# The sixteen experts of a routed layer taken in reverse order

## The chip, the cores and the metric

The kernel runs on one core of a Trainium2 chip. The metric is the device time of one launch in microseconds (us), the median of several launches. TensorE (PE) multiplies matrices, VectorE (DVE), ScalarE (ACT) and GpSimd (POOL) do the elementwise work, and DMA queues move data between HBM and on-chip memory. Each engine runs its own instructions in program order and waits at semaphores.

## The reference, cut to what matters

A block of three layers on 1,024 tokens of width 512 in float32: a cross attention, a self attention, and a mixture of experts. The change is in the last:

```python
scores = sigmoid(x @ gate_weight.T)              # 16 experts in 4 groups of 4
biased = scores + expert_bias                    # 2 of 4 groups by the sum of their two best
_, sel = top_k(where(group kept, biased, -inf), 4)   # 4 experts per token, ties to the lower number
w = 2.5 * scores[sel] / sum(scores[sel])
for e in range(16):                              # g, u: 256 x 512, d: 512 x 256
    y = (silu(x @ g[e].T) * (x @ u[e].T)) @ d[e].T
    out += w_of_e * y
out += shared expert                             # the same form, for every token
```

The inputs are drawn with a fixed seed, with a bias per expert that makes the load uneven. Working the routing out on them gives the number of tokens per expert:

| expert | 0 | 1 | 2 | 3 | 4 | 5 | 6 | 7 | 8 | 9 | 10 | 11 | 12 | 13 | 14 | 15 |
|---|---|---|---|---|---|---|---|---|---|---|---|---|---|---|---|---|
| tokens | 981 | 544 | 973 | 306 | 335 | 60 | 4 | 360 | 0 | 6 | 10 | 0 | 304 | 2 | 211 | 0 |
| tiles of 128 rows | 8 | 5 | 8 | 3 | 3 | 1 | 1 | 3 | 1 | 1 | 1 | 1 | 3 | 1 | 2 | 1 |
| tiles up to and with it | 8 | 13 | 21 | 24 | 27 | 28 | 29 | 32 | 33 | 34 | 35 | 36 | 39 | 40 | 42 | 43 |

An expert without tokens still gets one tile: the kernel counts an expert's tiles as the number of steps of 128 below its count, and the first step is written as -1.

## The kernel before, in words

The attention layers fill the first 1,080 us and are untouched. The last layer is `build_moe`, in two parts.

**Routing.** Eight groups of 128 tokens are projected, normalised and turned. For each, DVE works out which 4 experts every token takes: `route_groups` and `route_experts` count for each expert how many others are better, with `tri` (a 16 by 16 table of 0 and 1 in the constants `route_rows`) deciding ties. POOL then scatters each token's row to four places in an HBM buffer `xs`, in which every expert owns eight blocks of 128 rows. `table_cols` and `table_row` turn the counts into a table of 47 tiles (`tab`): for each tile the expert whose weights it needs, the place of these weights, and the block of `xs` to read. 47 is the most that can be needed; the tiles beyond the 43 real ones read and write spare blocks.

**The tile loop.** For each tile, in the order of the table, PE first waits for the tile's weights (`pe.wait_ge(w_ready, ready)`), then does the gate and up products (12 products of 512 columns on `XT`), in their midst turns the hidden rows of the tile before (`turn_h`) and the input rows of the next (`turn_x`), and then does the down products of the tile before (6 products of 512 columns). ACT and DVE split the operands into a high and a low part in between: DVE does `ht_low` (L1830), `xt_low` (L1820), `gated` (L1826) for each tile, and in tiles 8 to 16 also one step each of `sort_slots` (L1743 to L1755), which sorts each token's four places. SP writes each tile's result back to its block of `xs`. Below, tile i begins with the first of its gate products, an L64 row of PE, and "the ht_low of tile i" is DVE's L1830 of that tile, which runs within tile i + 1.

**Weights.** On-chip memory holds five experts (`NSLOT = 5`, slot e % 5). POOL brings them in by number: for each expert it waits until the expert five before it is through (`tile_done` against `cum_i`), makes the high part (L1523), the low part (L1480), raises `w_ready`, and issues the load of the expert two further on (L1484) into one of two raw buffers. Expert 0 is made by ACT and DVE before the loop; experts 2 to 4 need the shared expert's last product.

```python
pool.wait_ge(tile_done, pool.value_load(cum_i[0:1, e - NSLOT:e - NSLOT + 1], min_val=1,
                                        max_val=NTILE + 1))
...
pool.tensor_copy(slot(e)[0], raw[(e + 1) % 2]).then_inc(pool_hi, 1)
```

**The end.** After its last expert POOL issues 32 gathers (L1539): for k = 0 to 3 the row of each token's k-th expert in the order of number, eight groups of tokens each. The eight of one k wait until the tiles of expert 12 + k are written back, since a token's k-th expert can't have a higher number. DVE adds each gathered group to the output, weighted (`combine`, L1837): twelve of them within the last tiles, 20 after the `ht_low` of the last tile; SP then writes the eight output groups (L1454).

Of the kernel before, what the change touches and what calls it, by code (L numbers as in the profile page):

```python
# [25 lines left out]
ALU = mybir.AluOpType  # L26
# [29 lines left out]
NE, TOPK, NG, TOPG, I = 16, 4, 4, 2, 256  # L56
# [786 lines left out]
def wait(eng, sem, value):  # L843

    if not isinstance(value, int) or value > 0:
        eng.wait_ge(sem, value)
# [418 lines left out]
C_BIAS, C_TRI, C_TRIG, C_DIAG = 0, NE, NE + NE * NE, NE + NE * NE + NG * NG  # L1265
# [8 lines left out]
def _route_rows(bias):  # L1274

    tri = (np.arange(NE)[None, :] < np.arange(NE)[:, None]).astype(np.float32)
    tri_g = (np.arange(NG)[None, :] < np.arange(NG)[:, None]).astype(np.float32)
    slot = np.arange(NE) % NSLOT
    step = np.where(np.arange(NE) == NE - 1, 0, np.where(slot == NSLOT - 1, 1 - NSLOT, 1)) * SLOT
    real = (np.arange(NE) < NE - 1).astype(np.float32)  # L1280
    parts = [bias, tri.ravel(), tri_g.ravel(), -1e30 * np.eye(GS).ravel(), np.arange(TOPK), np.arange(NE) * T,
             np.arange(NT) * P - (np.arange(NT) == 0), step, real]
    return np.concatenate([np.asarray(p, np.float32) for p in parts]).reshape(1, C_END)


def build_moe(nc, ctx, sem, t, keep):
# [7 lines left out]
    def sb(name, shape, dt=F32):  # L1294
        return ctx.enter_context(nc.sbuf_tensor(name, shape, dt))
# [22 lines left out]
    masked, cmp_e, rank = sb("masked", [P, NE]), sb("cmp_experts", [P, NE, 2, NE]), sb("rank", [P, NE])  # L1318
# [20 lines left out]
    def c_row(at, n):  # L1339
        return con[:, at:at + n]  # L1340

    tri = c_row(C_TRI, NE * NE).rearrange("p (i j) -> p i j", j=NE)
    tri_g = c_row(C_TRIG, NG * NG).rearrange("p (i j) -> p i j", j=NG)
    diag = c_row(C_DIAG, GS * GS).rearrange("p (i j) -> p i j", j=GS)

    pb = [ctx.enter_context(nc.psum_tensor(f"bank{j}", [P, BANK], F32)) for j in range(8)]
# [8 lines left out]
    A = [early[:, j * nh * P:(j + 1) * nh * P].rearrange("p (h x) -> p h x", x=P) for j in range(2)]  # L1355
# [271 lines left out]
    def _(dve):  # L1627
        count = [0]

        def link(ins):  # L1630

            count[0] += 1
            ins.then_inc(route, 1)
            dve.wait_ge(route, count[0])

        def free(ins):

            count[0] += 1
            ins.then_inc(route, 1)
# [47 lines left out]
        def route_experts(tt):  # L1687
            j = tt % 2
            mj = masked[:].unsqueeze(1).to_broadcast([P, NE, NE])
            mi = masked[:].unsqueeze(2).to_broadcast([P, NE, NE])  # L1690
            free(dve.tensor_tensor(cmp_e[:, :, 0, :], mj, mi, ALU.is_gt))  # L1691
            link(dve.tensor_tensor(cmp_e[:, :, 1, :], mj, mi, ALU.is_equal))
            link(dve.tensor_tensor(cmp_e[:, :, 1, :], cmp_e[:, :, 1, :], tri, ALU.mult))
            link(dve.tensor_reduce(rank[:], cmp_e[:].rearrange("p i a j -> p i (a j)"), AX.X, ALU.add))
            wait(dve, prefix_mm, tt - 1)
            link(dve.tensor_scalar(sel[j][:], rank[:], float(TOPK), None, ALU.is_lt))
            wait(dve, prefix_mm, tt)
            dve.tensor_tensor(seen[1 - j][:], seen[j][:], sel[j][:], ALU.add).then_inc(sel_made, 1)
            link(dve.tensor_tensor(K[j][:], rank[:].unsqueeze(1).to_broadcast([P, TOPK, NE]),
                                   c_row(C_K, TOPK).unsqueeze(2).to_broadcast([P, TOPK, NE]), ALU.is_equal))  # L1700
            link(dve.tensor_tensor(kx[:], K[j][:], sig[:, tt, :].unsqueeze(1).to_broadcast([P, TOPK, NE]), ALU.mult))
            link(dve.tensor_reduce(wk[:], kx[:], AX.X, ALU.add))
            link(dve.tensor_reduce(wsum[:], wk[:], AX.X, ALU.add))
            link(dve.tensor_scalar(wsum[:], wsum[:], 1e-20, None, ALU.add))
            link(dve.reciprocal(wsum[:], wsum[:]))
            link(dve.tensor_scalar(cw[:, tt, :], wk[:], wsum[:, 0:1], SCALING, ALU.mult, ALU.mult))
# [71 lines left out]
        for tt in range(NT):  # L1778
            x2_stats(tt)
            if tt >= 2:  # L1780
                slots(tt - 2)
            norm(tt)
            if tt == NT - 1:
                break
            if tt >= 1:
                route_groups(tt - 1)
            h3_low(tt)
            if tt >= 1:
                route_experts(tt - 1)
            if tt == 1:  # L1790
                dve.wait_ge(sh_hi, 1)
                dve.tensor_tensor(WS[:, shared + wcol:shared + 2 * wcol], raw[0], f32(WS[:, shared:shared + wcol]),
                                  ALU.subtract).then_inc(sh_lo, 1)
        last = NT - 1
        h3_low(last)
        route_groups(last - 1)
        route_experts(last - 1)
        route_groups(last)
        product(0)
        route_experts(last)  # L1800
        product(1)
        hidden_low(0)
# [211 lines left out]
def build(nc, t):  # L2014

    outer = ExitStack()
    with outer:
# [37 lines left out]
        with ExitStack() as ctx:  # L2055
            build_moe(nc, ctx, sem, t, keep)
# [35 lines left out]
def _rows(w):  # L2092

    return w.T.reshape(w.shape[1] // P, P, w.shape[0]).transpose(1, 0, 2)
# [50 lines left out]
```

## Time and profile before

| | us |
|---|---|
| median of 3 runs | 1516.76 |
| lowest and highest | 1516.18, 1520.94 |
| the profiled execution | 1518.74 |
| its span, from the first to the last instruction | 1516.9 |
| mean granted TensorE clock over the span | 0.959 of full |

The profiled execution took 1.84 us more than its span, and 1.98 us more than the median. Times in the views are from the start of the span. Of the span, the last 433 us are `build_moe`'s, and the tile loop starts at 1247.58 us and ends with DVE's last `ht_low` at 1486.97 us.

### The profile page before, as it was taken

The page shows a single profiled execution, that of the slowest core. Times are in us where ns is not written, and L with a number is a line of the kernel's source. Part 1 is how long each engine was busy: PE and PEld are TensorE (multiplying, and loading weights), DVE is VectorE, ACT ScalarE, POOL GpSimd, SP SyncE. Part 2 cuts the span into 40 slices and gives each one's busy share as a digit, 9 for nine tenths or more (in the row PEclk, how much of TensorE's full clock was granted, in tenths as well). Part 3 has the DMA queues.
Part 4 walks back from the last instruction along what each step waited for, and adds up shares of the span by engine and source line. Part 5 has one row for each costly group of instructions (what it writes and reads, how often), then busy time and mean ns, then how long its engine had stood idle before and what let it go on. Part 6 is the DMA issues. An engine that isn't in the chain of part 4 may idle for free. (4 is left out here: it accounts for less than half of the span.)

```text
span 1516.9 us, 22837 instructions
## 1 busy us (share of the span) xinstructions
PE 1361.9 (90%) x7136; PEld 1105.5 (73%) x7136; DVE 809.9 (53%) x1371; ACT 734.6 (48%) x1741; POOL 573.7 (38%) x346
## 2 busy tenths in 40 slices
PE   5998699999999999999985899999689979999992
PEld 4776578777777777777764688888578768777781
DVE  4434365656566666666544444444479863433235
ACT  2444465655555555555533577777521213333330
POOL 2122333333333332333103233333246466517985
PEclk9999799999999999999997999999699999999996
DMA  5786540323232323232315111112544246446667
GB/s 192 244 274 184 221 153 29 136 87 124 97 124 97 124 97 124 97 124 97 135 60 190 62 50 63 49 48 98 190 163 142 84 174 215 155 139 219 232 205 232
DMA packets 78984, 209.79 MB, mean 138 GB/s; under 512 B 5888, under 2 KB 39168, under 8 KB 72960
## 3 DMA queue, kind: packets, MB, share of 16 engines
q1 hardware_dynamic: 69472, 163.78, 30.4%
q0 software_dynamic: 7136, 38.80, 7.7%
q10 hardware_dynamic: 2304, 6.29, 1.1%
q8 instruction: 40, 0.66, 0.2%
q14 instruction: 32, 0.26, 0.1%
HBM read 154.59 MB, written 92.01 MB: 163 GB/s over the span
## 5 line engine op out<-in xcount | busy, mean ns | idle before, releaser
L660 DVE TENSOR_TENSOR probsT_lo<-psTr,probsT_hi 128x512 fp32r<-128x512 f32 x256 | 176.5, 690 | 199.9 <-ACT probsT_hi L610 199.5
L610 ACT CAST probsT_hi<-psTr 128x512 fp32r<-128x512 f32 x256 | 149.8, 586 | 211.7 <-PE psTr L750 211.0
L750 PE MATMUL psTr<-ident,probs 128*128 128x128 f32 x1024 | 152.5, 276 | 18.6 <-DVE probsT_lo L660 12.4
L750 PEld LDWEIGHTS psTr<-ident,probs 128*128 128x128 f32 x1024 | 122.3, 141 | 62.0 <-DVE probsT_lo L660 28.8
L527 POOL TENSOR_TENSOR ctxT_lo<-ctx_f,ctxT_hi 128x512 fp32r<-128x512 f32 x32 | 41.3, 1290 | 321.1 <-ACT ctxT_hi L579 321.1
L655 DVE TENSOR_REDUCE nmax<-psS 128x1 f32<-128x1024 f32 x128 | 155.4, 1214 | 11.5 <-PE psS L66 10.7
L572 ACT ACTIVATE probs<-psS,nmax 128x1024 f32<-128x1024 f32 x128 | 143.3, 1120 | 28.2 <-DVE nmax L655 28.2
L64 PE MATMUL bank<-w_slots,ao_first_hi 128*128 (+1 forms) x252 | 107.8, 428 | 15.3 <-DVE w_slots L1774 9.4
L64 PE MATMUL psV<-probsT_hi,kv_hi 128*128 128x512 f32 x256 | 117.3, 458 | 2.0
L64 PE MATMUL psS<-kT_hi,qe 128*128 128x512 f32 x256 | 113.1, 442 | 5.5 <-issue 4.7
L1480 POOL TENSOR_TENSOR w_slots<-w_ahead,w_slots 128x3072 fp32r<-128x3072 f32 x15 | 102.5, 6836 | 1.2
L66 PE MATMUL psS<-kT_hi,qe 128*128 128x512 f32 x256 | 102.5, 400 | 0.0
L65 PE MATMUL psS<-kT_lo,qe 128*128 128x512 f32 x256 | 101.6, 397 | 0.0
L66 PE MATMUL psV<-probsT_hi,kv_lo 128*128 128x512 f32 x256 | 101.3, 396 | 0.0
L65 PE MATMUL psV<-probsT_lo,kv_hi 128*128 128x512 f32 x256 | 100.5, 392 | 0.0
L66 PE MATMUL bank<-w_slots,ao_first_lo 128*128 (+1 forms) x252 | 100.1, 397 | 0.0
L65 PE MATMUL bank<-w_slots,ao_first_hi 128*128 (+1 forms) x252 | 99.6, 395 | 0.0
L64 PE MATMUL bank<-w_slots 128*128 128x512 f32 (+1 forms) x206 | 84.9, 412 | 8.1 <-DVE w_slots L1830 4.4
L1186 PEld LDWEIGHTS psSs<-kTs,qT 128*128 128x128 f32 x512 | 76.4, 192 | 9.6
L1830 DVE TENSOR_TENSOR w_slots<-bank,w_slots 128x256 fp32r<-128x256 f32 x47 | 19.9, 424 | 117.0 <-ACT w_slots L1608 116.9
L66 PE MATMUL bank<-w_slots 128*128 128x512 f32 (+1 forms) x206 | 82.2, 399 | 0.0
L65 PE MATMUL bank<-w_slots 128*128 128x512 f32 (+1 forms) x206 | 82.0, 398 | 0.0
(268 smaller groups left out, 3328.8 us busy)
## 6 DMA issues: line engine op xcount, KB each, us to landing
w_ahead<-w_exp POOLq DMA_DIRECT2D x14, 1536.0 KB, 7.4
qe<-stage SPq DMA_DIRECT2D x16, 1024.0 KB, 6.7
qe<-qe SPq DMA_DIRECT2D x16, 1024.0 KB, 5.0
wraw<-w_pairs SPq DMA_DIRECT2D x8, 1792.0 KB, 11.3
early<-xs SPq DMA_DIRECT2D x47, 256.0 KB, 2.7
xs<-h_rows SPq DMA_DIRECT2D x47, 256.0 KB, 2.0
early<-ctx SPq DMA_DIRECT2D x16, 512.0 KB, 3.8
ao<-attn_out SPq DMA_DIRECT2D x32, 256.0 KB, 2.4
```

What stands on the lines that cost most here:

```text
L64: pe.matmul(out, lhs[0], rhs[0], start=start, stop=False, skip_group_check=True)
L65: pe.matmul(out, lhs[0], rhs[1], start=False, stop=False, skip_group_check=True)
L66: return pe.matmul(out, lhs[1], rhs[0], start=False, stop=stop, skip_group_check=True)
L527: pool.tensor_tensor(CT.lo[:, cols[0], cols[1]], CX[:].rearrange("p (h s) -> p h s", s=S), f32(CT.hi[:, cols[0], cols[1]]), ALU.subtract). ...
L572: act.activation(PR[np_][:, rt, :], psS[rt % 2][:], ACT.Exp, bias=nmax[np_][:, rt:rt + 1], accum_out=rsum[np_][:, rt:rt + 1]).then_inc(exp ...
L610: act.copy(PT[k % PTN].hi[:], psT[slot][:]).then_inc(turned_hi, 1)
L655: dve.tensor_reduce(nmax[np_][:, rt:rt + 1], psS[rt % 2][:], AX.X, ALU.max, negate=True).then_inc(max_made, 1)
L660: dve.tensor_tensor(out, psT[slot][:], f32(hi), ALU.subtract).then_inc(turned_free, 1)
L750: last = pe.transpose(psT[slot][:, q * P:(q + 1) * P], src(q), ident[:])
L1186: last = pe.matmul(psS[j][:, h, :], QB[j][:, h].rearrange("p b s -> p (b s)"), KB[kt][:, g, :], start=False, stop=h == REP - 1, skip_group ...
L1480: pool.tensor_tensor(slot(e)[1], raw[(e + 1) % 2], f32(slot(e)[0]), ALU.subtract).then_inc(w_ready, 1)
L1830: dve.tensor_tensor(HT[i % 2][1], psHT[i % 2][:, 0:I].rearrange("p (k x) -> p k x", k=NIT), f32(HT[i % 2][0]), ALU.subtract).then_inc(ht_l ...
```

## The change: experts in reverse order

The kernel's expert number j now stands for the reference's expert 15 - j: the weights, the router's columns and the bias are handed over reversed. So that ties still go to the same expert, the comparisons read the tie tables transposed. No instruction is added, removed or moved on any engine.

```diff
@@ build_moe
     tri = c_row(C_TRI, NE * NE).rearrange("p (i j) -> p i j", j=NE)
-    tri_g = c_row(C_TRIG, NG * NG).rearrange("p (i j) -> p i j", j=NG)
+    tri_after = c_row(C_TRI, NE * NE).rearrange("p (j i) -> p i j", j=NE)
+    tri_g = c_row(C_TRIG, NG * NG).rearrange("p (j i) -> p i j", j=NG)
...
@@ route_experts
-            link(dve.tensor_tensor(cmp_e[:, :, 1, :], cmp_e[:, :, 1, :], tri, ALU.mult))
+            link(dve.tensor_tensor(cmp_e[:, :, 1, :], cmp_e[:, :, 1, :], tri_after, ALU.mult))
...
@@ kernel
-    gates = np.concatenate([A(L0_ffn_shared_gate)[None], A(L0_ffn_gate_proj)])
-    ups = np.concatenate([A(L0_ffn_shared_up)[None], A(L0_ffn_up_proj)])
-    downs = np.concatenate([A(L0_ffn_shared_down)[None], A(L0_ffn_down_proj)])
+    gates = np.concatenate([A(L0_ffn_shared_gate)[None], A(L0_ffn_gate_proj)[::-1]])
+    ups = np.concatenate([A(L0_ffn_shared_up)[None], A(L0_ffn_up_proj)[::-1]])
+    downs = np.concatenate([A(L0_ffn_shared_down)[None], A(L0_ffn_down_proj)[::-1]])
...
-        "gate_w": _rows(A(L0_ffn_gate_weight)),
-        "route_c": _route_rows(A(L0_ffn_expert_bias)),
+        "gate_w": _rows(A(L0_ffn_gate_weight)[::-1]),
+        "route_c": _route_rows(A(L0_ffn_expert_bias)[::-1]),
```

The table of tiles that the device works out then reads, by the new numbers:

| expert | 0 | 1 | 2 | 3 | 4 | 5 | 6 | 7 | 8 | 9 | 10 | 11 | 12 | 13 | 14 | 15 |
|---|---|---|---|---|---|---|---|---|---|---|---|---|---|---|---|---|
| tiles | 1 | 2 | 1 | 3 | 1 | 1 | 1 | 1 | 3 | 1 | 1 | 3 | 3 | 8 | 5 | 8 |
| tiles up to and with it | 1 | 3 | 4 | 7 | 8 | 9 | 10 | 11 | 14 | 15 | 16 | 19 | 22 | 30 | 35 | 43 |

## Rows read from the trace of the kernel before

**Rows 1.** The page: busy us, share, instructions; then the chain that ended last.
```profile
PE 1361.9 (90%) x7136; PEld 1105.5 (73%) x7136; DVE 809.9 (53%) x1371; ACT 734.6 (48%) x1741; POOL 573.7 (38%) x346
...
PE bank L64 4%; PE bank L66 4%; PE bank L65 4%; POOL w_slots L1480 3%; POOL w_slots L1539 1%; POOL w_slots L1523 1%; PE bank L1950 1%; DVE cmp_experts L1691 1%; DVE h_rows L1660 1%; POOL w_ahead L1539 0%; PE bank L1981 0%; DVE st L1648 0%; DVE acc L1645 0%; DVE cmp_experts L1748 0%; DMA w_slots<-xs,slot_sorted_int 0%
```

**Rows 2.** Windows: stretch, its us, busy us (instructions) per engine, clock, DMA share.
```profile
1329.00:1487.00 158.00, 152.87 (x741) 122.44 (x739) 55.07 (x106) 59.51 (x124) 106.95 (x42) 0.99 0.60 201
1487.00:1517.00 30.00, 1.79 (x6) 1.06 (x6) 14.97 (x22) 0.58 (x1) 17.41 (x15) 0.53 0.74 228
```

**Rows 3.** Timeline of POOL, tile loop: start, us, work, idle before.
```profile
1246.22 2.74 POOL L1523 CAST w_slots<-w_ahead 128x3072 fp32r<-128x3072 f32 x1 [3.88 <-issue]
...
1256.70 2.77 POOL L1523 CAST w_slots<-w_ahead 128x3072 fp32r<-128x3072 f32 x1
...
1277.17 0.55 POOL L1484 DMA_DIRECT2D w_ahead<-w_exp  x1 [0.30 <-POOL w_slots L1480]
1290.95 2.75 POOL L1523 CAST w_slots<-w_ahead 128x3072 fp32r<-128x3072 f32 x1 [13.23 <-PE bank L66]
...
1358.25 2.75 POOL L1523 CAST w_slots<-w_ahead 128x3072 fp32r<-128x3072 f32 x1 [31.70 <-PE bank L66]
...
1387.43 2.75 POOL L1523 CAST w_slots<-w_ahead 128x3072 fp32r<-128x3072 f32 x1 [4.21 <-PE bank L66]
...
1422.81 6.78 POOL L1480 TENSOR_TENSOR w_slots<-w_ahead,w_slots 128x3072 fp32r<-128x3072 f32 x1
...
1441.20 2.75 POOL L1523 CAST w_slots<-w_ahead 128x3072 fp32r<-128x3072 f32 x1
...
1450.79 2.76 POOL L1523 CAST w_slots<-w_ahead 128x3072 fp32r<-128x3072 f32 x1
1453.63 6.86 POOL L1480 TENSOR_TENSOR w_slots<-w_ahead,w_slots 128x3072 fp32r<-128x3072 f32 x1
```

**Rows 4.** Timeline of PE: the first gate product of tiles 8, 16, 34 and 36.
```profile
1285.82 0.40 PE L64 MATMUL bank<-w_slots,ao_first_hi 128*128 x1
...
1328.36 0.49 PE L64 MATMUL bank<-w_slots,ao_first_hi 128*128 x1 [0.27 <-issue]
...
1417.79 0.40 PE L64 MATMUL bank<-w_slots,ao_first_hi 128*128 x1
...
1429.73 0.49 PE L64 MATMUL bank<-w_slots,ao_first_hi 128*128 x1 [2.08 <-POOL w_slots L1480]
```

**Rows 5.** Timeline of DVE: ht_low of tiles 7, 14, 15, 35, 36, and sort steps.
```profile
1288.04 0.42 DVE L1830 TENSOR_TENSOR w_slots<-bank,w_slots 128x256 fp32r<-128x256 f32 x1 [2.54 <-ACT w_slots L1608]
...
1295.14 0.28 DVE L1746 TENSOR_REDUCE slot_rank<-cmp_experts 128x32 f32<-128x128 f32 x1
...
1320.38 5.46 DVE L1748 TENSOR_TENSOR cmp_experts<-slot_rank,route_rows 128x128 f32<-128x128 f32 x1
1325.88 0.42 DVE L1830 TENSOR_TENSOR w_slots<-bank,w_slots 128x256 fp32r<-128x256 f32 x1
...
1330.73 0.42 DVE L1830 TENSOR_TENSOR w_slots<-bank,w_slots 128x256 fp32r<-128x256 f32 x1 [3.29 <-ACT w_slots L1608]
...
1432.60 0.42 DVE L1830 TENSOR_TENSOR w_slots<-bank,w_slots 128x256 fp32r<-128x256 f32 x1 [5.45 <-ACT w_slots L1608]
...
1438.44 0.42 DVE L1830 TENSOR_TENSOR w_slots<-bank,w_slots 128x256 fp32r<-128x256 f32 x1 [2.53 <-ACT w_slots L1608]
```

**Rows 6.** Windows, as in Rows 2, behind the wait of tile 36.
```profile
1430.00:1434.00 4.00, 4.00 (x15) 3.35 (x15) 0.75 (x2) 0.96 (x2) 3.78 (x3) 0.60 0.83 288
```

**Rows 7.** Timeline of POOL: the first and the last of the 32 gathers.
```profile
1461.93 1.04 POOL L1539 DMA_INDIRECT w_ahead<-xs,slot_sorted_int  x1 [1.44 <-issue]
...
1508.27 1.03 POOL L1539 DMA_INDIRECT w_slots<-xs,slot_sorted_int  x1 [0.30 <-issue]
```

**Rows 8.** Timeline of DVE: last ht_low, five additions in a row, the last addition.
```profile
1486.97 0.42 DVE L1830 TENSOR_TENSOR w_slots<-bank,w_slots 128x256 fp32r<-128x256 f32 x1
1487.31 3.40 DVE L1837 SCALAR_TENSOR_TENSOR acc<-w_slots,weight_sorted,acc 128x512 f32<-128x512 f32 x5
...
1513.45 0.75 DVE L1837 SCALAR_TENSOR_TENSOR acc<-w_slots,weight_sorted,acc 128x512 f32<-128x512 f32 x1 [0.52 <-DMA w_slots<-xs,slot_sorted_int]
```

**Rows 9.** Groups by line and form: busy us, mean ns, idle before.
```profile
L1693 DVE TENSOR_TENSOR cmp_experts<-cmp_experts,route_rows 128x256 f32<-128x256 f32 x8 | 3.4, 425 | 0.3
```

## The prediction

> **What bounds the kernel now.** I read the page first. PE is busy for 90% of the span, and the chain that ended last runs through PE's products, but three of POOL's lines are in it: the making of expert weights (L1523, L1480) and the gathers (L1539) [rows 1]. The windows say where. From 1329 to 1487 us, inside the tile loop, PE is busy 152.87 of 158 us; from 1487 us on it does 1.79 us of work in 30, while POOL and DMA work [rows 2]. So the loop is PE's, and the last 30 us are not.
>
> The timeline of POOL explains this end. With large experts in front, POOL waits for PE to free a slot: 13.23 us before expert 5 and 31.70 us before expert 7 [rows 3]. The small experts (numbers 8 to 11, a tile each) are used up faster than POOL makes weights. From expert 9 on it works without a break: expert 9 begins at 1387.43, expert 14 at 1441.20, expert 15 at 1450.79, and its low part ends at 1453.63 + 6.86 = 1460.49 [rows 3]. Only then come the gathers, the first at 1461.93 and the last at 1508.27 [rows 7], one every 46.34 / 31 = 1.49 us. DVE's last `ht_low` is at 1486.97, its last addition ends at 1513.45 + 0.75 = 1514.20, having waited for the gather [rows 8], and the span ends at 1516.9, 2.7 us later. From the last `ht_low` to the end it is 29.9 us, of which DVE adds for about half.
>
> **The change, part by part.** It issues nothing new. It changes the numbers in the tile table, and so who waits for whom. There are four terms.
>
> *The tie table.* L1693 runs eight times, 425 ns each [rows 9], and now reads the table with a stride of 16 elements. Nothing in the trace reads with this stride. The bounds are 0 and, if an element took twice the time, 8 x 0.42 = 3.4 us, all on DVE's path in the routing. The same line handles 256 elements in 0.42 us, one per 1.6 ns with its fixed cost, no faster form that the stride could spoil, so I take 0.
>
> *Starvation at the front of the loop.* The new order has 1, 2, 1, 3, 1, 1, 1, 1, 3, 1, 1 tiles for experts 0 to 10, so expert 11 is due at tile 16. POOL can start expert 5 at once, since expert 0's single tile is long done: at 1277.17 + 0.55 = 1277.72, where before it waited to 1290.95 [rows 3]; I take 1277.85 with the reading of the count. From there it never waits for a slot: expert e waits for the tiles of expert e - 5, for instance expert 11 for ten tiles, and these are through tens of us before it. The period, from start to start with the issue of a load, is (1441.20 - 1387.43) / 5 = 10.75 us [rows 3]. The shortest is 1256.70 - 1246.22 = 10.48. Expert 11 starts at 1277.85 + 6 x 10.75 = 1342.4, is ready 1453.63 + 6.86 - 1450.79 = 9.70 us after its start, at 1352.1, and PE starts 0.14 us after that (1429.73 against 1422.81 + 6.78 = 1429.59 [rows 3, 4]): tile 16 begins at 1352.2. Before, it began at 1328.36 [rows 4]. Hence **+23.8 us**.
>
> That tile 16 is the last that waits follows from the same sums: expert 12 is ready at 1362.8 for tile 19, which PE reaches at 1352.2 + 3 x 4.9 = 1366.9, and expert 13 at 1373.6 for tile 22. That the others don't add to it follows too. PE waits at tile 8 (expert 5 ready at 1287.6, PE there at about 1286 [rows 4]), and by about 5.8 us at each of tiles 9, 10 and 11, whose experts 6 to 8 come 10.75 us apart for one tile of 4.9 us; tile 11 begins at about 1319.9. From there to tile 16 it is five tiles, 24.5 us, in the 32.3 us that POOL takes for three experts: 7.8 us of slack, which must cover what follows.
>
> *Sort steps behind POOL.* In tiles 8 to 16 DVE does its sort steps. One of them, a product of two on-chip operands, took 5.46 us in place of 0.28 while POOL made a low part, and the next `ht_low` came at 1325.88, 7.67 us after the one before it in place of 4.9: 2.8 us lost [rows 5]. A reduction in the same position, with POOL in the midst of a low part, took 0.28 [rows 5]. So the steps that read two tensors (and the copy, for which I assume the same) wait for POOL's instruction to end, and PE loses what exceeds about 2.4 us. Before, POOL was idle in most of these tiles; now it is busy in all. Steps 3 and 5, in tiles 11 and 13, would lose 1 to 2 us each; step 7, in tile 15, ends with the same low part for which PE waits at tile 16. With the clock below this takes 4 to 5 of the 7.8 us of slack. **0 us**; uncovered they would cost up to 2.8 + 1.5 us.
>
> The Trainium skill (SBUF — State Buffer, Who interferes with whom) says that a Vector instruction with two on-chip inputs, or a copy in a two-port mode, and a GpSimd instruction exclude each other for their whole length, and that a reduction does not take part. The row of 5.46 us and that of 0.28 us agree; the copy isn't shown by a row here.
>
> *The clock after the wait.* PE idles some 3 us before tile 16. Behind the wait of tile 36 the granted clock was 0.60 over 4 us, that is, 1.2 GHz for most of them [rows 6]. The `ht_low` of tile 35 came 1432.60 - 1429.73 = 2.87 us after the tile's start, where at tile 8 it was 1288.04 - 1285.82 = 2.22, and the next 5.84 us later in place of 4.9 [rows 4, 5]: about **+1.5 us**, once, at tile 16. The earlier ones lie within waits for POOL.
>
> *From tile 16 to the last.* Before, this took 1486.97 - 1328.36 = 158.6 us. Tiles 16 to 34 took 89.4 us, 4.97 each; two tiles and a wait 11.9 us; from tile 36 to the last `ht_low` 57.2 us [rows 4, 8]. The wait at tile 36 and its slow clock are gone: expert 12 is now early. That is 11.9 - 9.8 = 2.1, and 1.5 of clock, **-3.6 us**. Tiles 16 to 34 ran with weight loads beside most of them; now loads end by about 1373. I take **-1.4 us** (0 to -2). So the last `ht_low` comes at 1352.2 + 158.6 + 1.5 - 3.6 - 1.4 = 1507.3, which is **+20.3 us**.
>
> *The end.* POOL makes its last weights by about 1395 and issues the gathers of k = 0 then. Those of k = 1, 2 and 3 wait for tile 29, 34 and 42 to be written back. Tile 42 is written back about 9 us after tile 43 starts (down products, ACT's copy, SP's write), at about 1494, and eight gathers at 1.49 us end by 1506, before DVE's last `ht_low`. The additions then wait for nothing: 20 of them at 3.40 / 5 = 0.68 us [rows 8], 13.6 us, then 2.7 us as before. The end comes 0.34 + 13.6 + 2.7 = 16.6 us after the last `ht_low`, 16.8 with some queueing of eight writes issued 0.68 us apart, in place of 29.9: **-13.1 us**.
>
> The sum is +20.3 - 13.1 = +7.2 us, which I round down to +7.0, since the period may lie nearer to 10.5. The span becomes 1523.9 and its execution 1525.7. Against the median of 1516.76, which lies 1.98 below the profiled execution, it is **1523.8 us**.
>
> The Trainium skill (Perfetto Trace Analysis, GPSIMD Engine Instruction) warns against the durations that a profile gives for GpSimd and advises the spacing of starts. By the durations alone an expert is 2.75 + 6.82 us, six of them 57.4 in place of 64.5, and the sum would be about 0. The spacing of 10.75 us contains the issue of a load and its idle gaps, and decides here.
>
> **Rivals.** A difference within 0.3%, 4.5 us, is about what a measurement of this kernel can't tell from no change.
>
> *The period is shorter, or the loop makes up more.* At 10.48 us tile 16 comes 1.6 us earlier; with no slow clock there, 1.5 us more, and with 4.85 us per tile behind it 0.6 more: +3.3, 1520.1. For it: 10.48 us was measured at the start of this very stretch [rows 3]. Against: the mean of five later periods is 10.75. With no gap at all, 9.6 us, the sum is 0. Chance 0.19.
>
> *The slack is not enough.* If the sort steps and slow clocks between tiles 11 and 16 take more than 7.8 us, or PE loses the clock for longer, or the stride costs, each adds on top: +4 on average, +11, 1528. For it: POOL is busy all the time there, and the steps come at an unknown phase of it. Chance 0.18.
>
> *The end isn't shortened.* If the gathers of the last expert still ended last, only the +20.3 would be left: 1537. It takes 13 us more than I find between the last write-back and the additions. Chance 0.03.
>
> *The other side: PE is never starved.* If POOL's weights were ready in time, only the end would change, by -13.1 (and -3.6 for tile 36): 1500 to 1504. It decides once expert 11 takes POOL below 8.5 us each, where POOL's two instructions alone take 9.6. As an escape from my sum, a gain needs 11.5 us less than I find in front. Chance 0.05.
>
> My forecast, +4.6 to +10, has the remaining 0.55. Slower holds 0.55 + 0.18 + 0.03 = 0.76, less a little at the edge: 0.75; same 0.20; faster 0.05. The range reaches down into the short period, 1518, and up over the lost slack, 1531.5.
>
> **What would show it.** POOL's casts for experts 5 to 15 follow each other every 10.5 to 10.9 us with no wait for PE, the last low part ending near 1395. PE waits for L1480 about six to eight times, by over 4 us at tiles 9, 10 and 11 and by 2 to 4 at tile 16, whose first product is near 1352; none after it. The granted clock drops between 1290 and 1360. The last `ht_low` is at 1505 to 1509, the gathers end before it, and the additions behind it stand without idle time. L1693 still takes 425 ns. The prediction is wrong if POOL's period changes with PE's idleness, if a sort step holds PE past tile 16, if PE's rate behind tile 16 differs from before, or if the routing before 1247 shifts.

## The result and the profile after

| | before | after |
|---|---|---|
| median, us | 1516.47 | 1537.66 |
| lowest and highest | 1515.16, 1520.94 | 1534.44, 1541.47 |
| profiled execution, its span | 1518.74, 1516.9 | 1535.88, 1534.1 |

The ratio is 1.013, with a 95% interval of 1.0099 to 1.0161: slower by 21 us, where the forecast was 7 and the range ended at 1531.5. Lines of the kernel after carry numbers one higher than before (`ht_low` L1831, low part L1481, cast L1524, gather L1540).

The page of after, as [rows 1] of before. POOL's low part now has 4% of the chain, before 3%, and the gathers are no longer among the lines shown:

```profile
PE 1374.0 (90%) x7136; PEld 1112.5 (73%) x7136; DVE 825.9 (54%) x1371; ACT 735.2 (48%) x1741; POOL 572.0 (37%) x346
...
POOL w_slots L1481 4%; PE bank L64 4%; PE bank L66 4%; PE bank L65 4%; POOL w_slots L1524 2%; PE bank L1951 1%; DVE cmp_experts L1692 1%; DVE h_rows L1661 1%; PE bank L1982 0%; DVE acc L1838 0%; DVE st L1649 0%; DVE acc L1646 0%; DVE w_slots L1775 0%; DVE w_slots L1766 0%
```

Windows of after, columns as in [rows 2], cut at the first `ht_low`, at that of tile 15, at the last, and at the end:

```profile
1257.20:1358.70 101.50, 80.96 (x360) 63.68 (x359) 45.48 (x53) 28.99 (x60) 95.86 (x30) 0.92 0.64 222
1358.70:1517.80 159.10, 152.22 (x732) 121.24 (x730) 55.06 (x106) 58.63 (x123) 68.23 (x42) 0.99 0.54 173
1517.80:1534.10 16.30, 1.63 (x6) 1.06 (x6) 13.65 (x21) 0.59 (x1) 0.00 (x0) 0.68 0.44 162
```

In the first stretch POOL is busy 95.86 of 101.5 us and PE waits for it: this stretch took 77.2 us before (from `ht_low` 1253.57 to that at 1330.73 [rows 5]). In the third DVE adds without a pause and POOL does nothing, where the same end took 29.9 us.

The timeline of POOL after, as [rows 3] and [rows 7]: the casts of experts 5 and 11, the last low part, the first and the last gather.

```profile
1281.89 2.75 POOL L1524 CAST w_slots<-w_ahead 128x3072 fp32r<-128x3072 f32 x1 [0.46 <-issue]
...
1345.85 2.75 POOL L1524 CAST w_slots<-w_ahead 128x3072 fp32r<-128x3072 f32 x1 [0.72 <-issue]
1348.68 6.76 POOL L1481 TENSOR_TENSOR w_slots<-w_ahead,w_slots 128x3072 fp32r<-128x3072 f32 x1
...
1390.51 6.83 POOL L1481 TENSOR_TENSOR w_slots<-w_ahead,w_slots 128x3072 fp32r<-128x3072 f32 x1
1398.78 1.04 POOL L1540 DMA_INDIRECT w_ahead<-xs,slot_sorted_int  x1 [1.44 <-issue]
...
1510.67 0.96 POOL L1540 DMA_INDIRECT w_slots<-xs,slot_sorted_int  x1 [0.30 <-issue]
```

The period is (1345.85 - 1281.89) / 6 = 10.66 us, and no cast waits for PE. The timeline of PE has the first product of tile 16, as [rows 4], and the waits of PE over the whole loop (us, times, longest) name the cause:

```profile
1355.58 0.49 PE L64 MATMUL bank<-w_slots,ao_first_hi 128*128 x1 [3.10 <-POOL w_slots L1481]
```
```profile
PE bank L64 <- POOL w_slots L1481: 17.3, 6, 5.5
PE bank L64 <- DVE w_slots L1831: 6.5, 2, 3.8
```

The timeline of DVE, as [rows 5] and [rows 8]: sort steps beside POOL's low parts, then the last tiles and the additions.

```profile
1296.13 6.03 DVE L1744 TENSOR_TENSOR cmp_experts<-slot_all 128x128 f32<-128x128 f32 x1
...
1308.05 0.28 DVE L1747 TENSOR_REDUCE slot_rank<-cmp_experts 128x32 f32<-128x128 f32 x1
...
1327.70 6.12 DVE L1752 TENSOR_TENSOR cmp_experts<-cmp_experts,slot_all 128x128 f32<-128x128 f32 x1
...
1342.23 2.08 DVE L1756 CAST slot_sorted_int<-slot_sorted 128x32 int32<-128x32 f32 x1
...
1358.73 0.42 DVE L1831 TENSOR_TENSOR w_slots<-bank,w_slots 128x256 fp32r<-128x256 f32 x1 [3.15 <-ACT w_slots L1609]
...
1504.07 0.42 DVE L1831 TENSOR_TENSOR w_slots<-bank,w_slots 128x256 fp32r<-128x256 f32 x1
...
1513.36 0.42 DVE L1831 TENSOR_TENSOR w_slots<-bank,w_slots 128x256 fp32r<-128x256 f32 x1 [4.42 <-ACT w_slots L1609]
...
1517.78 0.42 DVE L1831 TENSOR_TENSOR w_slots<-bank,w_slots 128x256 fp32r<-128x256 f32 x1 [1.02 <-ACT w_slots L1609]
1518.12 13.33 DVE L1838 SCALAR_TENSOR_TENSOR acc<-w_slots,weight_sorted,acc 128x512 f32<-128x512 f32 x20
```

Two `ht_low` near the end are 1513.36 - 1504.07 = 9.3 us apart in place of 4.8. ACT's timeline has the wait in front of it, which the view can't put down to an instruction of the program ("remote"). ACT waits there for the hidden rows of this tile to be turned, and PE's own row of that work stands more than 4 us earlier:

```profile
1508.31 0.38 PE L1982 MATMUL bank<-ident,early 128*128 128x128 f32 x2
...
1512.95 0.37 ACT L1609 CAST w_slots<-bank 128x256 fp32r<-128x256 f32 x1 [5.55 <-remote]
```

The semaphore events kept with the trace say the same. The one that PE raises behind this work came at 1512.93, where the record of the work ends at 1508.70, and the one behind the last gate product came at 1513.00, where its record ends at 1510.09. So what was late was PE's result or its signal, and not a transfer that ACT waited for. Why, the trace doesn't show. The ends of PE's records are modelled.

And the group of the tie product, as [rows 9]:

```profile
L1694 DVE TENSOR_TENSOR cmp_experts<-cmp_experts,route_rows 128x256 f32<-128x256 f32 x8 | 4.8, 605 | 0.3
```

The span grew by 17.2 us in four pieces: the first `ht_low` came 1257.17 - 1253.57 = 3.6 later; tile 16 began 1355.58 - 1328.36 = 27.2 later, that is 23.6 more; from there to the last `ht_low` it was 162.2 in place of 158.6, 3.6 more; the end was 13.6 shorter.

### The profile page after: what moved, and what is told of

Read it like the earlier page. It is cut to its first block and busy times, and to the rows that moved or that the text cites. A ratio compares the mean times of both kernels' runs of the same rounds, so it can differ in the third digit from the quotient of the medians.

```text
span 1534.1 us, 22837 instructions
## 1 busy us (share of the span) xinstructions
PE 1374.0 (90%) x7136; PEld 1112.5 (73%) x7136; DVE 825.9 (54%) x1371; ACT 735.2 (48%) x1741; POOL 572.0 (37%) x346
## 5 line engine op out<-in xcount | busy, mean ns | idle before, releaser
L64 PE MATMUL bank<-w_slots,ao_first_hi 128*128 (+1 forms) x252 | 110.1, 437 | 31.3 <-POOL w_slots L1481 17.3
L1481 POOL TENSOR_TENSOR w_slots<-w_ahead,w_slots 128x3072 fp32r<-128x3072 f32 x15 | 102.2, 6810 | 1.2
L65 PE MATMUL bank<-w_slots,ao_first_hi 128*128 (+1 forms) x252 | 101.6, 403 | 0.0
L66 PE MATMUL psS<-kT_hi,qe 128*128 128x512 f32 x256 | 101.5, 396 | 0.0
L64 PE MATMUL bank<-w_slots 128*128 128x512 f32 (+1 forms) x206 | 86.0, 417 | 11.6 <-DVE w_slots L1831 7.7
L1831 DVE TENSOR_TENSOR w_slots<-bank,w_slots 128x256 fp32r<-128x256 f32 x47 | 20.0, 425 | 125.4 <-ACT w_slots L1609 119.8
L64 PEld LDWEIGHTS bank<-w_slots,ao_first_hi 128*128 128x128 f32 x252 | 49.1, 195 | 51.7 <-issue 44.4
L66 PE MATMUL bank<-w_slots 128*128 128x512 f32 (+1 forms) x206 | 82.8, 402 | 0.0
```

The source lines that it names most:

```text
L64: pe.matmul(out, lhs[0], rhs[0], start=start, stop=False, skip_group_check=True)
L65: pe.matmul(out, lhs[0], rhs[1], start=False, stop=False, skip_group_check=True)
L66: return pe.matmul(out, lhs[1], rhs[0], start=False, stop=stop, skip_group_check=True)
L1481: pool.tensor_tensor(slot(e)[1], raw[(e + 1) % 2], f32(slot(e)[0]), ALU.subtract).then_inc(w_ready, 1)
```

## The experiments

The loop starts at different times in executions of one and the same kernel (the first `ht_low` at 1253.6 in before, but between 1247.9 and 1257.8 in the runs below), so I compare the stretch *L* from the first `ht_low` to the end of the span: 263.3 us in before, 276.9 in after. Ratios are against runs of the kernel before on the same chip. All `ht_low` times are from DVE's timeline. *L* varies too: with the order of before it was 263.3 us in before and 266.4 in the tables alone, so a difference of *L* between two single traces is good to about 3 us.

**The tables alone.** The kernel before with the transposed reads and nothing reversed.

```diff
+    tri_after = c_row(C_TRI, NE * NE).rearrange("p (j i) -> p i j", j=NE)
...
-            link(dve.tensor_tensor(cmp_e[:, :, 1, :], cmp_e[:, :, 1, :], tri, ALU.mult))
+            link(dve.tensor_tensor(cmp_e[:, :, 1, :], cmp_e[:, :, 1, :], tri_after, ALU.mult))
```

> The kernel before with only the tie tables read transposed (exact ties between experts go to the higher number). First theory: the table read with a stride of 16 elements costs 0.18 us in each of eight routing steps (0.606 against 0.425 us each), so the time is 1 to 2 us above before, and the tile loop starts 1 to 2 us later. Rival: the whole 3.6 us by which the changed kernel's tile loop started later comes from these reads, directly and by what queues behind them: 3 to 4 us above before. Second rival: neither, the start of the loop varies between executions by that much: no difference.

Measured: ratio 1.0005 (0.9983 to 1.0026). The product took 606 ns in place of 425. The stride does cost, 8 x 0.18 = 1.45 us, but that is less than a measurement of the whole can show.

**The tables stored the other way.** The kernel after, with the constants transposed so that L1694 reads without a stride; only `table_cols` then reads a tie table with one, once. (A second copy of the table beside the first does not fit in on-chip memory.)

```diff
-    parts = [bias, tri.ravel(), tri_g.ravel(), -1e30 * np.eye(GS).ravel(), np.arange(TOPK), np.arange(NE) * T,
+    parts = [bias, tri.T.ravel(), tri_g.T.ravel(), -1e30 * np.eye(GS).ravel(), np.arange(TOPK), np.arange(NE) * T,
...
-    tri_after = c_row(C_TRI, NE * NE).rearrange("p (j i) -> p i j", j=NE)
+    tri_after = c_row(C_TRI, NE * NE).rearrange("p (i j) -> p i j", j=NE)
...
```

> The changed kernel with the tie tables stored transposed, so that the routing reads them in order of address and only table_cols reads one with a stride, once. First theory (the stride costs 0.18 us in each of eight steps): L1694 back at 0.425 us, the tile loop starts 1 to 2 us earlier than in the changed kernel, time 1 to 2 us below it. Rival (the start of the loop varies by itself): no difference that can be measured.

The group of the product in this kernel:

```profile
L1694 DVE TENSOR_TENSOR cmp_experts<-cmp_experts,route_rows 128x256 f32<-128x256 f32 x8 | 3.4, 425 | 0.3
```

Ratio 1.0038 (1.0017 to 1.0058), L = 270.9. The 1.5 us of the stride are back in the row; the ratio can't be told from that of the kernel after on the same chip, which comes next.

**The kernel after again, on chips B and C.** No edit. (The chip of the first result isn't recorded; the tables alone, the mixed order's first run and the faster POOL in the reversed order ran on a chip A. The tables stored the other way, the late sort steps and the faster POOL in the order of before ran on chip B, and the last batch, from the second run of the mixed order on, on a chip D.)

> The changed kernel once more, with a trace of its own. If the time behind tile 16 (162 us to the last ht_low, where 155 were forecast) belongs to the order, it is 160 us or more again, with the same slow tiles beside the gathers; if the tile of 9.3 us at the end is an accident of one execution, it is 155 to 158 us. Ratio to before 1.010 to 1.016 in either case.

On chip B: 1524.4 us (12 runs, 1520.24 to 1528.21), ratio 1.0029 (1.0011 to 1.0047), L = 269.6. The ratio is below what I expected in either case. The end of DVE's timeline there:

```profile
1500.56 0.41 DVE L1831 TENSOR_TENSOR w_slots<-bank,w_slots 128x256 fp32r<-128x256 f32 x1
...
1505.54 0.42 DVE L1831 TENSOR_TENSOR w_slots<-bank,w_slots 128x256 fp32r<-128x256 f32 x1
...
1509.93 0.42 DVE L1831 TENSOR_TENSOR w_slots<-bank,w_slots 128x256 fp32r<-128x256 f32 x1
```

The tile of 9.3 us is one of 5.0, and no wait in this trace is put down to "remote". From the `ht_low` of tile 15 to the last it is 1509.93 - 1357.96 = 152.0 us, where after had 1517.78 - 1358.73 = 159.1.

> The changed kernel a third time. Its first four executions took 1534 to 1541 us, twelve later ones 1520 to 1528 us beside 1519 us before. Theory (the first four held delays of 5 to 15 us that are not the order's): 1.001 to 1.006 of before again, every piece of the profile as in the second look, 253 to 257 us from the first ht_low to the last. Rival (the order does cost 1.3%, and the second look was the exception): 1.010 to 1.016.

On chip C: 1534.47 us (4 runs, 1533.01 to 1535.88), ratio 1.0097 (1.0073 to 1.0121). Its trace repeats the end of the first one: `ht_low` at 1504.04 and 1513.36, ACT's cast at 1512.95 after 5.58 us of "remote", 158.8 us from tile 15 to the last. Two tiles near 1470 are long in both (5.6 and 5.3 us). Others differ: beside the first eight gathers it was 5.45 and 5.36 us in the first result, 5.17 and 4.81 here; beside the next eight it was 5.07 and 5.00 there, 5.56 and 5.46 here. The theory fails, and the ratio comes close to the rival's 1.010. So the order comes with some 7 us more behind tile 16 in the first result and on chip C, and without them on chip B.

**One gather on its way.** In the loop, several tiles of after that were long for no wait on POOL lie beside gathers. `ON_WAY` sets how many of them may be on their way, for k = 0, 1 and 2 alone: the last eight gathers go out as before, 1.3 us apart.

```diff
-ON_WAY = 3
+ON_WAY = 1
```

> The changed kernel with one gather on its way at a time in place of three, for k = 0, 1 and 2. These 24 gathers have 13 to 28 us of idle POOL behind each eight, so spreading them costs nothing. Theory of a contention (gathers beside the tiles delay the writes and loads of tiles, which in the first profile made tiles of 5.3 to 5.6 us at 1405 to 1415 and 1465 to 1475): 1 to 4 us below the changed kernel. Rival (the gathers within the loop are hidden): no difference that can be measured.

Measured on chip C, beside the run just told: 1529.0 us (7 runs, none over 1531.31), ratio 1.0061 (1.0043 to 1.0079), L = 270.4. That is 5.5 us less than the kernel after on this chip, more than the 1 to 4 expected. DVE's timeline of the kernel after on chip C beside the second eight gathers:

```profile
1438.42 0.42 DVE L1831 TENSOR_TENSOR w_slots<-bank,w_slots 128x256 fp32r<-128x256 f32 x1 [2.58 <-ACT w_slots L1609]
1443.98 0.42 DVE L1831 TENSOR_TENSOR w_slots<-bank,w_slots 128x256 fp32r<-128x256 f32 x1 [1.58 <-ACT w_slots L1609]
1449.44 0.42 DVE L1831 TENSOR_TENSOR w_slots<-bank,w_slots 128x256 fp32r<-128x256 f32 x1 [3.72 <-ACT w_slots L1609]
```

and the same tiles on the same chip with one gather at a time:

```profile
1436.98 0.42 DVE L1831 TENSOR_TENSOR w_slots<-bank,w_slots 128x256 fp32r<-128x256 f32 x1 [2.61 <-ACT w_slots L1609]
1441.80 0.42 DVE L1831 TENSOR_TENSOR w_slots<-bank,w_slots 128x256 fp32r<-128x256 f32 x1 [2.56 <-ACT w_slots L1609]
1446.59 0.42 DVE L1831 TENSOR_TENSOR w_slots<-bank,w_slots 128x256 fp32r<-128x256 f32 x1 [2.53 <-ACT w_slots L1609]
```

Tiles of 5.56 and 5.46 us have become 4.82 and 4.79. From tile 15 to the last it is 152.7 us in place of 158.8, and this gain of 6.1 us has two parts. From the `ht_low` of tile 15 to that of tile 44 it went from 145.1 to 141.8, and 3.0 of these 3.3 us lie behind the first gather, where the edit spaced the gathers out. The last two tiles went from 13.7 to 11.0 (9.3 and 4.4 became 4.9 and 6.1), but the eight gathers beside them were not spaced out, and on chips B and D the same two tiles took 9.3 to 9.5 us with gathers as dense. So the late tile of 9.3 us can't be put down to gathers by this run.

The waits of ACT put down to "remote" fit this. There are five in the first result (14.3 us) and five in the kernel after on chip C (13.0 us), every one within one of the four bursts of gathers. With one gather at a time there is one, of 3.81 us, beside the last eight:

```profile
1509.96 0.58 ACT L1614 COPY h_rows<-bank 128x512 f32<-128x512 f32 x1 [3.81 <-remote]
```

No other trace of this document has one in its loop, and three gathers on their way are in most of them. So dense gathers stand beside each of these delays, but they don't bring them by themselves.

**The sort steps taken away from the starved tiles.**

```diff
-SORT_AT = 8
+SORT_AT = 22
```

> The changed kernel with the nine sort steps in tiles 22 to 30 in place of 8 to 16, most of them after POOL has made its last expert. Forecast's theory (the slack between POOL's experts covers the sort steps): within 2 us of the changed kernel, tile 16 still starts 0.1 us behind expert 11's low part. Rival (the steps held by POOL push the loop): 3 to 8 us below the changed kernel, and tile 16 no longer waits for its weights only.

Measured: ratio 1.0051 (1.0032 to 1.007), on chip B, where the kernel after had 1.0029. From the first `ht_low` to that of tile 15 it is 102.1 us, with the steps in these tiles 101.4: they cost nothing there, since POOL ends later than they do. Moved, one of them made a tile of 7.6 us where nothing hides it, and the kernel took 1527.75 us, 3.4 more than the kernel after on this chip, where I expected less than 2. The forecast's 0 us for them was right.

**POOL made faster.** The low part is made for half of an expert's columns alone (the other half keeps what was in the slot, so this kernel leaves out part of the computation), in the kernel after and in that before.

```diff
-            pool.tensor_tensor(slot(e)[1], raw[(e + 1) % 2], f32(slot(e)[0]), ALU.subtract).then_inc(w_ready, 1)
+            n = wcol // 2
+            pool.tensor_tensor(slot(e)[1][:, 0:n], raw[(e + 1) % 2][:, 0:n], f32(slot(e)[0][:, 0:n]),
+                               ALU.subtract).then_inc(w_ready, 1)
```

> The changed kernel with the low part of every expert from number 1 on made for the first half of its columns only (left out: the correction of the other half of the weights). POOL then needs 2.75 + 3.4 us per expert. Theory (PE starves because POOL makes an expert every 10.7 us): the period falls to 7.5 to 9 us, where the load of the next expert becomes the limit, tile 16 starts 10 to 18 us earlier, and the kernel takes 1518 to 1528 us. Rival (the loop is late for another reason, such as sort steps behind POOL or slow tiles late in the loop): less than 5 us are gained.

> The kernel before with the low part of every expert from number 1 on made for the first half of its columns only (left out: the correction of the other half of the weights), as in e3_half_low. Theory (the order only decides when POOL is late): POOL makes an expert in 7.5 us, so the last one is ready some 20 us earlier, tile 36 does not wait, and the gathers start when their tiles are written back; the last ht_low is near 1484 us and 20 to 24 us lie behind it, 1504 to 1510 us in all, and the reversed order with the same edit (span 1506.4) is within 5 us of it. Rival (the reversed order has a shorter end whatever POOL's speed): the reversed order stays 10 us or more below this one. Rival (the reversed order is slower in the loop whatever POOL's speed): it stays 5 us or more above.

Reversed: 1517.47 us (10 runs, 1508.22 to 1522.56), ratio 0.9961 (0.9935 to 0.9987); a period of 7.2 to 8.9 us; 81.9 us from the first `ht_low` to that of tile 15, in place of 101.6 in after; L = 250.5. The time lies just below the 1518 to 1528 expected. Not reversed: 1504.55 us (5 runs), ratio 0.9908 (0.9875 to 0.994); 73.3 us for the same tiles; an end of 27.2 us, where 20 to 24 were expected; L = 251.7. So 101.6 - 81.9 = 19.7 us of the reversed kernel's front go with POOL's speed: it is POOL that starves PE. The 8.5 us that stay have another cause. Waits of PE in the reversed one (us, times, longest), 1250 to 1345 us:

```profile
PE bank L1953 <- DMA early<-xs: 5.9, 3, 4.0
```

Its window, columns as in [rows 2]:

```profile
1255.90:1337.70 81.80, 75.84 (x361) 61.12 (x361) 33.53 (x53) 28.79 (x61) 72.73 (x32) 0.96 0.83 289
```

PE waits for the rows of the next tile, not for weights: with the weight loads closer together DMA is busy 0.83 of this stretch, where it was 0.64 in after. And the whole L of the two is equal within 1.2 us, while their ratios are 0.5% apart on two chips; the profiled execution of the first was the fastest of its ten. Whether reversing gains anything with a faster POOL stays open.

**Another order.** If starvation comes from many small experts in a row, and the long end from small experts last, an order with large ones in between avoids the first and keeps part of the gain of the second.

```diff
+    ORDER = [12, 13, 14, 15, 0, 1, 2, 3, 8, 9, 10, 11, 4, 5, 6, 7]
-    gates = np.concatenate([A(L0_ffn_shared_gate)[None], A(L0_ffn_gate_proj)])
+    gates = np.concatenate([A(L0_ffn_shared_gate)[None], A(L0_ffn_gate_proj)[ORDER]])
...
```

> The kernel before with the experts in the order 12 to 15, 0 to 3, 8 to 11, 4 to 7: tiles 3 1 2 1, 8 5 8 3, 1 1 1 1, 3 1 1 3. Eight tiles lie behind the last burst of small experts and PE never waits long in front. Theory: no starvation (POOL is ahead by the large experts and five slots), and the last gathers wait only for tile 42, so both terms of the end are kept: the last ht_low at 1484 to 1490 us and 16.5 us behind it, 1500 to 1507 us in all. Rival (any order whose last experts end late makes tiles slower in the loop by gathers beside them, 5 to 7 us): 1506 to 1513. Rival (the end is not shortened by an order, only by chance): as before, 1515 to 1520.

Measured: 1506.38 us (4 runs), ratio 0.988 (0.9843 to 0.9917), L = 251.3. PE's waits over its whole loop:

```profile
PE bank L64 <- DVE w_slots L1830: 2.8, 2, 2.4
PE bank L64 <- issue: 1.9, 6, 0.4
PE bank L64 <- POOL w_slots L1480: 1.6, 1, 1.6
```

POOL holds PE for 1.6 us, where it was 17.3 in after. Its last low part ends at 1451.1, where it was 1460.5 in before, so the end takes 22.1 us in place of 29.9. That is less of a gain than the 16.5 us that I expected behind the last `ht_low`: the gathers still end last here. From the first `ht_low` to the last it is 229.2 us (before 233.4, after 260.6).

> The order 12-15, 0-3, 8-11, 4-7 once more, unchanged, on another chip perhaps. Theory (this order keeps half of the shorter end without starving PE long, and few gathers fall beside its tiles): ratio 0.985 to 0.991, as before, 251 us from the first ht_low to the end. Rival (its first result was a happy chip, as the reversed order's differ by 0.7% between chips): ratio 0.994 or more.

Again, on chip D: 1505.1 us (6 runs), ratio 0.9903 (0.9876 to 0.9929), L = 251.0. It holds.

**Both together, and what is left of the order.**

> The order 12-15, 0-3, 8-11, 4-7 with one gather on its way at a time in place of three. Theory (in the reversed order it was the gathers issued beside the tiles that made tiles long, and few of them fall beside tiles here): the tiles beside the gathers, at about 1453 to 1487 us, go by 4.9 us each, some 1 to 3 us sooner than with three on the way; the end behind the last ht_low is the same 22 us or up to 3 us longer, since gathers one by one take longer; time 1502 to 1507, ratio 0.985 to 0.990. Rival (the gathers behind the last low part set the end of this kernel, so spacing them out costs all of it): last gather at 1505 or later in place of 1500, time 1510 or more, ratio 0.993 or more.

Measured: 1561.78 us, ratio 1.0284 (1.0254 to 1.0314). The rival was right, and by far. POOL's timeline of this kernel:

```profile
1495.64 1.35 POOL L1539 DMA_INDIRECT w_slots<-xs,slot_sorted_int  x1 [2.71 <-DMA w_slots<-xs,slot_sorted_int]
1500.16 1.35 POOL L1539 DMA_INDIRECT w_slots<-xs,slot_sorted_int  x1 [3.17 <-DMA w_slots<-xs,slot_sorted_int]
1504.03 1.35 POOL L1539 DMA_INDIRECT w_slots<-xs,slot_sorted_int  x1 [2.52 <-DMA w_slots<-xs,slot_sorted_int]
```

They start 4.1 us apart on the average, in place of 1.6 us in this order with three on their way. 24 of them are spaced so, they begin when the last weights are made (1442.35), and the last addition waits for them: an end of 64.2 us. In the reversed order they had some 110 us of tiles to hide behind, here 50.

> The changed kernel with both of what it can be relieved of: tie tables stored transposed and read without a stride, and one gather on its way in place of three. Theory (stride 1.5 us, gathers beside tiles up to 5.5 us, the rest is the order's own price of +20 to +24 in front of tile 16 and -13 at the end): 268 to 270 us from the first ht_low to the end, time +4 to +8 against the kernel before, ratio 1.003 to 1.005. Rival (each of the two reliefs only shifts where PE waits): as the changed kernel, 272 us or more from the first ht_low, ratio 1.007 or more.

Measured: 1523.87 us (12 runs), ratio 1.0034 (1.0016 to 1.0052), L = 269.5. Without the stride and with 24 of the 32 gathers spaced out, the reversed order costs 269.5 - 263.3 = 6.2 us in *L*, good to about 3 us, and 5.5 us in the medians of this chip. That is what the order itself costs, as far as these runs tell. The unrelieved kernel did not run on chip D; on chip B its L was 269.6, so there three gathers on their way cost nothing that can be seen.

## Why the prediction was wrong

**The starved front: right.** Forecast +23.8 at tile 16 from a period of 10.75; measured 10.66 and, counted from the first `ht_low`, +23.6. PE waited six times for L1481; the last of them, 3.10 us, was at tile 16, as said, where "some 3 us" stood. Of the waits of over 4 us that I named at tiles 9, 10 and 11, the third was 2.58. Faster POOL took 19.7 us of it away. One figure among the rivals is off: 8.5 us per expert would still starve PE. Tile 16 at 1328.36 asks for seven periods less 1.05 us from 1277.85 on, that is 7.4 us each. The sum doesn't use it. The spacing of starts decided, not the durations, as the sentence on the Trainium skill (Perfetto Trace Analysis, GPSIMD Engine Instruction) said.

**The end: right.** 16.3 us against 16.8, that is -13.6 against -13.1. POOL was through with issuing gathers at 1511.6, before the last `ht_low`, and the additions behind it waited for none.

**The sort steps: right in sum.** Steps on two tensors took up to 6.12 us, reductions 0.28. The copy, which I had only assumed to behave the same, took 2.08 us, where it was 0.17 in before, and ended at 1344.31, with POOL's low part (1337.48 + 6.79 = 1344.27). The rule of the Trainium skill (SBUF — State Buffer, Who interferes with whom) covers it; this trace agrees. None of it reached tile 16: the step of 6.12 us made PE wait 2.7 us at tile 12, inside the slack.

**The clock behind the wait: right.** The `ht_low` of tile 15 came 3.15 us after the start of tile 16 and the next 5.61 us later, in place of 2.22 and 4.9: 1.6 us against 1.5.

**The tie table: mis-sized.** Forecast 0, measured 1.45 us, inside the bounds of 0 to 3.4. My reason (no faster form that a stride could spoil) was wrong: 256 elements took 0.18 us more.

**"From tile 16 to the last": the step that failed.** I took +1.5 us of slow clock, -3.6 and -1.4, so 155.1 us in place of 158.6. Measured in the first result: 162.2, so 7.1 us off. On chip B the term held: from the `ht_low` of tile 15 to the last 152.0 us, where the forecast was 155.1 less the 3.15 from the start of tile 16 to that `ht_low` (1358.73 - 1355.58), 151.9. What I had left out stands in my own part on the end: all 32 gathers move from behind the last tiles to beside them, and I costed them there at nothing. For that I gave no reason, though the rows of before would have agreed: its tiles 40 to 45, beside gathers, took 4.8 to 4.9 us. What the runs showed in its place is, for the first result, 4.3 us more in the last two tiles and about 2.7 more in the tiles up to 44, both against chip B. On chip C spacing out 24 of the gathers took away 3.0 us in the tiles beside them, which shows a cost of about that size there, by one trace against one and with medians 5.5 us apart. It also found the last two tiles 2.7 us shorter, though the gathers beside those were left as they were. So the 9.3 us tile stays open: PE's result or its signal came 4.2 us late, in two traces, at the same instruction, beside gathers as dense as those that did no harm on chips B and D. Through which resource the gathers act isn't shown: they write on-chip memory and read the buffer `xs` that SP writes. Nor is it known why one chip shows it and another doesn't.

**The start.** Of the 3.6 us by which the profiled execution began its loop later, the stride explains 1.5; the rest is within the 10 us by which this start differs between executions of all kernels.

The sum, then: the order costs 5 to 7 us, near the 7 forecast, by the medians (5.2 us for the kernel after on chip B, 5.5 for the relieved one on chip D) and by *L* (6.2 to 6.3 us), and gives a ratio of 1.003 to 1.004 where nothing else comes (1.0029 and 1.0038 on chip B, 1.0034 on chip D). The first result has more: L grew by 13.6 us, of which 6.3 are those of chip B (269.6 - 263.3) and 7.3 come almost all behind tile 16, as told; the loop began 3.6 us later; and the medians are 4 us further apart than the two profiled executions, since that of before lay 2.3 above its median and that of after 1.8 below. The last two pieces are within the spread of the executions, and they add as much to the miss of 13.9 us (1537.66 against 1523.8) as the failed step. The rival "the end isn't shortened" gave 1537, the right time by the wrong mechanism: the end was shortened by all that I said.

## What to carry to other kernels

When an order of unequal jobs is changed, work out both ends: small jobs at the front starve the consumer by (period of the producer - time of a job) each, small jobs at the end push back what waits for the producer. These are estimates; the first held here to 0.2 us and the second to 0.5. Mixing them, with the producer's head start spent on large jobs, beat the first order here by 1.0 to 1.2%, and the reversed one by more. And a transfer that moves from behind the work to beside it is not free because nobody waits for it. The tiles that stood beside gathers before the change showed no price, and nor did chip B: it took a second and a third chip to see one. Where a difference of 1% matters, measure both kernels on more than one chip.

## What the runs showed of the hardware

- The same program took 0.3% more than its predecessor on chip B and 1.0% more on chip C. The trace of chip C and that of the first result (1.3%) have their longest delay at the same tile (9.3 us in place of 5.0).
- In these two traces ACT got PE's result of that tile at 1512.93 us, 4.2 us after PE's record of it ends; on chip B it got it 0.02 us after.
- Gathers of 128 rows by an index list: 3.8 to 4.1 us apart on the average of eight when each waits for the one before to land, 1.3 to 1.6 us with three on their way.
- A VectorE product of 256 elements in float32 took 606 ns with one operand read at a stride of 16 elements, 425 ns without.
- With weights made every 7.2 to 8.9 us in place of 10.6, loads of 256 KB that the next tile needs came late by up to 4.0 us.
